# Attention stage of a fused kernel: ScalarE copies the turned heads before it computes the root, and VectorE takes three of the norm's four steps after its maxima

## What is computed

```
field = (zX, zY, zR) mix of y and its second differences     # elementwise, and a matmul with a 256x256 matrix
x     = field / sqrt(mean(field^2) + eps) * g                # the norm: "squares", "root", "normalize"
q,k,v = x @ W_qkv ; q,k rotated                               # 16 heads of 64
P     = softmax(q k^T, inside segments of 128 tokens, plus 16 persistent keys)
y     = y + (P v) @ W_out
```

## Time and profile before

| | |
|---|---|
| median of three runs | 2478.77 us (2477.14 to 2478.88) |
| the profiled execution | 2469.4 us, span of its instructions 2467.7 us |
| TensorE busy | 2331.6 us, 94% of the span |
| VectorE busy | 1839.8 us, 75% |
| ScalarE busy | 1275.7 us, 52% |
| GpSimd busy | 1035.7 us, 42% |
| mean granted TensorE clock | 0.979 of full |
| stage C | about from 740 to 1590 us of the span |

### The profile page before, as it was taken

How to read it: one execution, slowest core, us unless ns; L and a number is a source line. 1 busy time by engine, 2 the same in 40 slices (tenths; PEclk the granted TensorE clock), 3 DMA queues, 4 the chain that set the end, 5 groups by cost and what they waited for, 6 DMA issues and landing times.

```text
span 2467.7 us, 55054 instructions
## 1 busy us (share of the span) xinstructions
PE 2331.6 (94%) x19136; PEld 2088.6 (85%) x19136; DVE 1839.8 (75%) x5136; ACT 1275.7 (52%) x3807; POOL 1035.7 (42%) x1090
## 2 busy tenths in 40 slices
PE   4899999999987799999999999899999999999999
PEld 3677887878876678888888887799999999999999
DVE  6777777777777766666666665578878888888876
ACT  2666666566554355555555555333325555555522
POOL 4645545446443545545545545123322222222063
PEclk7999999999998899999999999899999999999999
DMA  4311211211120221221222122122116777677443
GB/s 115 115 44 46 59 45 43 52 46 51 44 86 10 63 56 44 49 56 45 48 56 49 46 54 64 49 69 44 42 35 232 237 231 241 229 231 238 149 121 123
DMA packets 153080, 225.73 MB, mean 91 GB/s; under 512 B 54294, under 2 KB 123174, under 8 KB 142054
## 3 DMA queue, kind: packets, MB, share of 16 engines
q1 hardware_dynamic: 143942, 203.56, 28.2%
q0 software_dynamic: 8864, 18.66, 2.8%
HBM read 159.32 MB, written 27.16 MB: 76 GB/s over the span
## 4 chain that ended last, share of the span: by engine, by line
PE 69%; DVE 13%; POOL 7%; issue 5%; ACT 5%; DMA 1%; SPq 0%; POOLq 0%; DVEq 0%; ACTq 0%
PE bank L55 54%; PE bank L136 7%; PE bank L339 2%; POOL P L1743 2%; PE bank L1252 2%; PE bank L366 1%; PE bank L1292 1%; ACT Ph L621 1%; DVE xe L884 1%; ACT PTh L633 1%; POOL Qn L1768 1%; POOL Qn L1766 1%; DVE tb L1606 1%; DVE Ph L770 1%; POOL xr_lo L1775 1%
## 5 line engine op out<-in xcount | busy, mean ns | idle before, releaser
L1447 ACT ACTIVATE P<-P,mx 128x144 f32<-128x144 f32 x512 | 206.2, 405 | 263.7 <-DVE mx L1568 262.7
L2579 POOL DMA_INDIRECT xE<-d_y,ixs x78 | 111.7, 1432 | 336.2 <-PE bank L136 306.1
L55 PE MATMUL bank<-xD_hi,w1e_lo 128*128 128x256 f32 x880 | 251.1, 285 | 0.0
L55 PE MATMUL bank<-w2e_hi,hrD_hi 128*128 128x256 f32 x880 | 249.0, 283 | 0.0
L55 PE MATMUL bank<-w2e_lo,hrD_hi 128*128 128x256 f32 x880 | 248.9, 283 | 0.0
L55 PE MATMUL bank<-w2e_hi,hrD_lo 128*128 128x256 f32 x880 | 248.9, 283 | 0.0
L1743 POOL TENSOR_TENSOR P<-P,rs 128x512 f32<-128x512 f32 x128 | 133.1, 1040 | 275.2 <-DVE rs L1577 271.7
L55 PE MATMUL bank<-xD_lo,w1e_hi 128*128 128x256 f32 x880 | 245.9, 279 | 0.0
L55 PE MATMUL bank<-xD_hi,w1e_hi 128*128 128x256 f32 x880 | 245.6, 279 | 0.0
L1078 POOL TENSOR_TENSOR xe<-xe 128x704 f32<-128x704 f32 (+3 forms) x64 | 88.4, 1381 | 373.4 <-DVE xe L889 373.1
L2188 ACT ACTIVATE hD<-bank,b1E 128x256 f32<-128x256 f32 x312 | 126.9, 473 | 197.3 <-PE bank L55 188.0
(11 more groups left out here) (324 smaller groups left out, 7990.6 us busy)
## 6 DMA issues: line engine op xcount, KB each, us to landing
w1raw<-in_ew SPq DMA_DIRECT2D x39, 1024.0 KB, 5.8
w2raw<-in_ew SPq DMA_DIRECT2D x39, 1024.0 KB, 4.8
K<-Kn SPq DMA_DIRECT2D x256, 72.0 KB, 2.1
Q<-Qn SPq DMA_DIRECT2D x256, 64.0 KB, 2.0
d_ys<-oE SPq DMA_DIRECT2D x39, 256.0 KB, 2.4
d_rot<-QK SPq DMA_DIRECT2D x16, 512.0 KB, 2.9
Rs<-d_rot SPq DMA_DIRECT2D x64, 128.0 KB, 4.2
b2E<-in_eb SPq DMA_DIRECT2D x39, 128.0 KB, 3.5
```

The source lines that it names most:

```text
L55: inst = e.matmul(out, l, r, start=k == 0, stop=k == len(pairs) - 1)
L1447: inst = e.activation(P1[t % 2][:, n, :], P1[t % 2][:, n, :], ACT.Exp, bias=mx1[t % 2][:, 2 * g + sg:2 * g + sg + 1], scale=-1.0, accum_ou ...
L2579: e.indirect_dma_start(out=xE[q % 2][c], out_offset=None, in_=d_y, in_offset=bass.IndirectOffsetOnAxis(ap=ixs[r % 4][:, c:c + 1].bitcast(U ...
```

## The change

In ScalarE's step 3 `root` moves behind `copy_turned`. On VectorE `normalize` is cut in two: its first instruction, with its waits, becomes `sums` and stays in front of step 4's `maxima`; the other four instructions keep the name `normalize` and come behind `maxima`, in front of `add_back`. No instruction is added or removed, and no wait.

```diff
@@ act_c
                     if b == -3 and s == 6:
                         x_high(0)
-                    if s == 3:
-                        root(entering(b))
                     if s == 7:
                         values_copy(b + 1, 0, 1)
                     copy_turned(t)
+                    if s == 3:
+                        root(entering(b))
                     if s == 2:
                         square(entering(b))
@@ dve_c
-            def normalize(b):
+            def sums(b):
+
                 if not 0 <= b < B:
                     return
                 e.wait_ge(c_rt, 2 * b + 2)
@@
                 e.scalar_tensor_tensor(out=rn1, in0=sums_bank(b), scalar=256.0 * EPS, in1=rt1,
                                        op0=ALU.add, op1=ALU.mult).then_inc(v_rn, 1)
+
+            def normalize(b):
+                if not 0 <= b < B:
+                    return
                 e.wait_ge(v_rn, 2 * b + 1)
@@
                     if b == -3 and s == 5:
+                        sums(0)
                         normalize(0)
@@
                     if s == 4:
-                        normalize(entering(b))
+                        sums(entering(b))
                     if s == 5:
                         rotate(b + 1, 5)
                     if s == 6:
                         rotate(b + 1, 7)
                     maxima(t + 1)
                     if s == 4:
+                        normalize(entering(b))
                         add_back(b - 1)
```

## The result

| | before | after |
|---|---|---|
| median of 22 runs each | 2478.36 us | 2481.48 us |
| ratio to before | | 1.0016, 95% interval 1.001 to 1.0022 |
| one batch of stage C (start of the root's reader L1649 / L1650 to the next, mean of 12) | 45.94 us | 46.27 us |
| that reader in batches 0 to 15, first to last | 717.35 us | 721.30 us |
| span of the profiled execution | 2467.7 us | 2480.0 us |

The kernel became 0.16% slower. Of the 12.3 us between the two profiled spans, 3.95 us lie between the first and the last reader of the root; 2.3 us lie ahead of the first and some 6 us behind the last, in code that is the same but for the end of one step. Inside the 3.95 us, too, the stretch from the reader of batch 0 to that of batch 1 is the same code: it took 79.02 us before and 78.61 after, and between 77.27 and 79.22 in the twelve traces of this document.

What follows compares the result with a forecast made beforehand. TensorE sets the pace, reached through VectorE's queue from root to project 5. Root +0.43 and VectorE's order -0.13 give +0.30 us a batch; 13 batches add 3.9 to 2478.8: 2482.7 us, range 2474.5 to 2487.0.

Steps and rivals of the forecast that it cites:

- What bounds the step: Step 4: root, norm, maxima and add_back in a row hold project 5, TensorE's last wait; the 0.36 us copy wait isn't last.
- Root's delay: ScalarE, step 3: root's first table load waits for the last copy's end, so root and sums come 0.43 us later.
- The copy's gain: TensorE, step 4: with PmT copied 3.5 us earlier, values and project 4 come 0.36 us earlier.
- VectorE's new order: VectorE, step 4: maxima overlap sums, so sums to add_back takes 2.95 us instead of 3.08, -0.13 us.
- Project 5: TensorE, step 4: its wait for add_back's X grows from 0.36 to 1.02 us, taking 0.30 us more per batch.
- Nothing absorbs it: After step 4: everything later hangs on project 5 or the invert, both 0.30 us late, until the next root.
- b = 0: First such batch, without add_back: no net change, bounds -0.6 us (L1652 clear of GpSimd) and +2.5 us (longer half clock).
- The sum: Whole kernel: 13 batches x 0.30 us = +3.9 us, with bounds including the first such batch from 1.6 to 8.1 us.
- the delay counts in full: Rival: VectorE gains no 0.13 us and half clock lasts longer in the first such batch; +8.1 us, 2486.9 us; chance 0.21.
- it does nothing: Rival: something else holds L1649 or project 5 anyway and covers the copies' 0.43 us; 2478.8 us; chance 0.10.
- TensorE keeps what the copy gives it: Rival: add_back doesn't hold project 5, so 0.36 to 0.72 us a batch is won; 2474.1 to 2469.4 us; chance 0.12.
- Drain: Rival: table loads behind the copies drain every batch, making sums later still; 2499.3 us, +20.5 us; chance 0.03.

Runs made afterwards that it cites:

- e1: Kernel before with only ScalarE's half of the change (copy_turned ahead of root in step 3): ratio to before 1.0021, batch 46.39 us.
- e6: Changed kernel with one extra ScalarE copy between copy_turned and root in step 3: ratio to before 1.0041, batch 46.56 us.
- e11: e9 with root ahead of copy_turned again in step 3: ratio to before 0.9979, batch 45.34 us.
- e2: Kernel before with only VectorE's half of the change (sums, maxima, normalize, add_back): ratio to before 0.9994, batch 45.83 us.
- e3: Changed kernel with add_back ahead of the rest of the norm in step 4: ratio to before 1.0018, batch 46.28 us.
- e9: Changed kernel with the norm's rest split, refining in step 6, applying in step 7; x_high and x_low moved to step 7: ratio to before 0.9965, batch 44.99 us.
- e4: Changed kernel with the rest of the norm moved from step 4 to behind step 5's maxima: ratio to before 1.0113, batch 47.76 us.
- e8: Changed kernel with the norm's rest whole behind step 7's invert, x_high and x_low moved to step 7: ratio to before 1.0066, batch 46.44 us.

## Why the prediction was right

The forecast was 2482.7 us, 0.16% over before; measured were 2481.48 us and 1.0016. The mechanism held, with one term of the sum too small that doesn't reach the total. Point by point:

- **What bounds the step.** That project 5, held by VectorE's queue, ends TensorE's last wait, and not the copy: the wait for PmT (0.36 us) went and the time didn't fall. e1, e6 and e11 confirm it from three sides.
- **Root's delay.** Forecast 0.43 us, measured 0.46 (VectorE's wait went from 2.92 to 3.38): the first copy takes 0.38 instead of 0.36, and the second starts 0.28 us behind it. The bound of 0.17, a load that needn't wait for the copy's end, is refuted.
- **The copy's gain.** Forecast -0.36 us, measured -0.53: the values start 0.59 us behind the first scores matmul instead of 1.12. The row's 0.36 us counts only from the modelled end of the matmul ahead. Nothing of this reaches the batch, since project 5 waits anyway.
- **VectorE's new order.** Forecast -0.13 us from sums to add_back, measured -0.12 in the trace after and -0.13 in e2, whose batch fell by 0.11.
- **Project 5.** Forecast a growth from 0.36 to 1.02 us, by the weight loads; by the weight loads it is 1.22. The 0.20 too few are the copy's gain (0.53 instead of 0.36) and the batch's 0.33 instead of 0.30. That the matmul's row shows 0.98 us is another measure, and its nearness to 1.02 is luck. The forecast also let project 4 wait for nothing. With TensorE earlier than foreseen it does wait for sums, 0.27 us by its weight load where such a load usually has 0.17, some 0.1 us more.
- **The batch.** Forecast +0.30 us, measured +0.33.
- **Nothing absorbs it.** e3 shows other ways at work: X's wait gone, the batch unchanged. The nearest of them, VectorE's own copy in the same queue, is one that the prediction didn't name.
- **b = 0.** Forecast no net change within -0.6 and +2.5. TensorE's idle time there grew to 3.89 us (it ends in the first row below). The granted clock fell to 0.50 inside it, 2.3 us before it ended, and stayed there for 6.8 us, as long as before; VectorE's L1657 had its 0.42 us. It starts as GpSimd's long multiply ends (874.14 + 1.04); the short one that begins beside it took 0.38 us instead of 0.29. Timelines of TensorE, VectorE and GpSimd, then windows (busy us per engine, granted clock), which answer to the earlier trace rows:

```profile
874.36 0.58 PE L55 MATMUL bank<-xr_hi,w_lo 128*128 128x256 f32 x1 [3.89 <-DVE rn L1650]
875.12 0.42 DVE L1657 SCALAR_TENSOR_TENSOR rn<-rn,fu 128x256 f32<-128x256 f32 x1
875.32 0.38 POOL L1755 TENSOR_TENSOR Pm<-P,rs 128x64 f32<-128x64 f32 x1
870.50:872.00 1.50, 0.00 (x0) 0.00 (x0) 0.00 (x0) 1.48 (x2) 0.00 (x0) 1.00 0.46 109
872.20:874.30 2.10, 0.00 (x0) 0.00 (x0) 1.09 (x4) 1.94 (x5) 0.16 (x1) 0.50 0.47 114
872.40:877.30 4.90, 2.94 (x14) 2.94 (x15) 4.02 (x16) 3.46 (x12) 1.42 (x2) 0.50 0.44 105
```

  From the reader of batch 1 to that of batch 3, which stands in step 4 of b = 1, it is 87.46 us after and 87.08 before. Of these 0.38 us, 0.46 are the later place of that reader in its own step, so b = 0 itself changed by -0.1 us: no net change, as forecast.
- **The sum.** Forecast 13 x 0.30 = 3.9 us. Like for like it is 13 x 0.33 = 4.3 us and the -0.1 of b = 0. The 3.95 us of the table are 12 batches (3.97), 0.38 for the stretch around b = 0 and -0.41 for the stretch in which nothing was changed; that they meet the forecast so closely is luck. The medians' 3.1 us are a little less than either, and no run shows where the rest went.

Of the rivals, "the delay counts in full" fell with the 0.33 us of the batch and with e2, and "it does nothing" with the batch and with the interval, 1.001 to 1.0022. "TensorE keeps what the copy gives it" came true only in e9 against e11, where the queue it needed was short. "Drain" fell: the load starts 0.02 us behind the copy. Here the trace differs from the Trainium skill, "ScalarE: Activation LUTs", section "What ACT_TABLE_LOAD costs", whose 1380 ns of drain appear in no row.

One thing that the prediction left out mattered only for what came next: it named GpSimd's idleness in step 4 as cover and stopped there. It was the reason why the norm was cheap in that place. The Trainium skill, "SBUF — State Buffer", section "Who interferes with whom", has the rule that a VectorE instruction with two SBUF inputs contends with a GpSimd one that reads SBUF. e4, e8 and e9 agree with it: the two refining steps, 0.42 us each, become 0.58 to 0.87, and the pair that applies the norm goes from 0.88 to 1.41 (e9), 1.58 (e8) and 1.72 (e4).

## What to carry to other kernels

When two waits of the bounding engine follow each other, find out which of them comes last, and whose queue ends it: work taken from in front of the first only lengthens the second if it is put in front of what ends that one. A delay on an in-order queue that feeds two engines can't be cured at one of them; shorten the queue, and then the edit that lost may win. Before moving elementwise work into another engine's gap, look at what GpSimd does at that time, and cut the work to the size of the gaps. And when a kernel is much slower than its queues explain, as in e4, look at the granted clock batch by batch before you put the whole difference down to the queue.

## What the runs showed of the hardware

- VectorE's instructions with two SBUF inputs (128x256) took 0.42 us, or 0.48 for the two that apply the norm, with GpSimd idle. Beside its tensor operations (e4, e8 to e11) they took 0.51 to 1.15 us, and one at b = 0 of the kernel before 1.12; GpSimd's combines grew from 0.74 to 0.80 us. At b = 0 of the changed kernel the VectorE instruction began first and kept its 0.42 us, while GpSimd's short multiply beside it took 0.38 instead of 0.29. Maxima, which read PSUM, stayed at about 0.30 us throughout, also beside GpSimd's multiply in e9. That the two engines' sharing is the cause is argued from where the rows lie; no run had GpSimd taken away.
- ScalarE's table load waits for the whole end of the copy or accumulator read ahead of it, in all eleven kernels that have one (it starts 0.01 to 0.02 us behind), though copies among themselves overlap by 0.10 us or so.
- TensorE's idle times of 0.98 us, 13 times in the changed kernel, left the granted clock at 1.00. Those of 1.75 to 1.81 us in e8 were followed by 0.50 for 3.4 us in 2 of 14 cases, those of 1.82 to 1.91 us in e4 in 12 of 13. In the idle times at b = 0, 3.05 us before and 3.89 after, it fell to 0.50 before they ended and stayed there for 6.8 us. No run varies the idle time alone, so no rule follows.
